# Time mixing from a difference made once a sequence on GpSimd, in a two-layer kernel (time-mixing attention and a mixture of experts)

## The reference

```python
x = x + attn(layernorm(x))      # time mixing, below
x = x + ffn(layernorm(x))       # convolution, 8 experts (top 2), rms norm, gelu feed-forward

xx = pad(x, one token at the front)[:, :-1, :]        # the token ahead
xk = x * time_mix_k + xx * (1.0 - time_mix_k)
xv = x * time_mix_v + xx * (1.0 - time_mix_v)
xr = x * time_mix_r + xx * (1.0 - time_mix_r)
k, v, r = xk @ Wk.T, xv @ Wv.T, xr @ Wr.T
rwkv = sigmoid(r) * wkv(w, time_first, k, v)          # a running, weighted mean over time
return rwkv @ Wo.T
```

## Time and profile before

| What | Value |
|---|---|
| Median of 3 runs | 1038.97 us (1038.87 to 1040.74) |
| Profiled execution, first to last instruction | 1038.4 us |
| TensorE busy | 955.6 us (92%) |
| VectorE busy | 863.5 us (83%) |
| ScalarE busy | 722.8 us (70%) |
| GpSimd busy | 207.7 us (20%) |
| Mean granted TensorE clock | 0.968 |

### The profile page before, as it was taken

How to read it: one execution, slowest core, us unless ns; L and a number is a source line. 1 busy time by engine, 2 the same in 40 slices (tenths; PEclk the granted TensorE clock), 3 DMA queues, 4 the chain that set the end, 5 groups by cost and what they waited for, 6 DMA issues and landing times.

```text
span 1038.4 us, 15789 instructions
## 1 busy us (share of the span) xinstructions
PE 955.6 (92%) x4288; PEld 470.2 (45%) x4288; DVE 863.5 (83%) x1577; ACT 722.8 (70%) x1233; POOL 207.7 (20%) x475
## 2 busy tenths in 40 slices
PE   4536999999999999999999999999999999979895
PEld 2222454454545545454444445444454545344432
DVE  4998889889898988989898888989898997957562
ACT  4664687786868787786868778686877779464532
POOL 3393302121131202112130222113120111101000
PEclk9766999999999999999999999999999999999997
DMA  6110100101010010101010010101001000100000
GB/s 198 42 40 1 41 1 1 62 1 62 0 61 0 23 38 0 61 0 61 0 57 4 0 61 0 61 0 61 0 8 53 19 24 1 41 1 21 1 21 20
DMA packets 28772, 29.66 MB, mean 29 GB/s; under 512 B 2090, under 2 KB 28484, under 8 KB 28484
## 3 DMA queue, kind: packets, MB, share of 16 engines
q1 hardware_dynamic: 28740, 29.27, 8.4%
HBM read 20.87 MB, written 8.39 MB: 28 GB/s over the span
## 4 chain that ended last, share of the span: by engine, by line
PE 81%; DVE 6%; POOL 5%; issue 4%; ACT 3%; DMA 0%; POOLq 0%; DVEq 0%; ACTq 0%; SPq 0%
PE pk L447 15%; PE pe L464 12%; PE pe L466 10%; PE pe L465 10%; PE pe L462 7%; PE po L507 6%; PE po L533 5%; PE pt L441 4%; PE pt L621 3%; POOL msp L408 1%; PE po L504 1%; PE po L501 1%; PE pt L486 1%; DVE comb L1292 1%; ACT sq L746 1%
## 5 line engine op out<-in xcount | busy, mean ns | idle before, releaser
L726 ACT ACTIVATE ye<-pe 128x512 f32<-128x512 f32 x256 | 152.7, 597 | 165.5 <-PE pe L466 152.3
L1292 DVE SCALAR_TENSOR_TENSOR comb<-ye,rw,comb 128x256 f32<-128x256 f32 x448 | 216.3, 483 | 44.9 <-ACT ye L726 30.8
L464 PE MATMUL pe<-weh,x1h 128*128 128x512 f16 x512 | 196.8, 384 | 0.0
L465 PE MATMUL pe<-wel,x1h 128*128 128x512 f16 x512 | 194.0, 379 | 0.0
L466 PE MATMUL pe<-weh,x1l 128*128 128x512 f16 x512 | 194.0, 379 | 0.0
L406 POOL TENSOR_TENSOR msv<-ms,rms_eps_c 128x2 f32<-128x2 f32 x32 | 11.4, 356 | 453.1 <-ACT sq L746 453.1
L462 PE MATMUL pe<-brow,ones 2*128 2x512 f16 x256 | 98.5, 385 | 0.0
L464 PEld LDWEIGHTS pe<-weh,x1h 128*128 128x128 f16 x512 | 49.5, 97 | 88.2 <-issue 58.0
L377 POOL TENSOR_TENSOR mo<-st 128x4 f32<-128x4 f32 x32 | 11.2, 348 | 339.1 <-DVE st L1098 181.8
L466 PEld LDWEIGHTS pe<-weh,x1l 128*128 128x128 f16 x512 | 50.1, 98 | 60.5
L447 PE MATMUL pk<-xk,wa 128*128 128x512 f32 x128 | 65.2, 657 | 11.3 <-issue 8.5
(11 more groups left out here) (152 smaller groups left out, 1946.7 us busy)
## 6 DMA issues: line engine op xcount, KB each, us to landing
xa<-in_x SPq DMA_DIRECT2D x16, 512.0 KB, 3.6
xres<-in_x SPq DMA_DIRECT2D x16, 512.0 KB, 4.4
out_y<-yo SPq DMA_DIRECT2D x16, 512.0 KB, 2.9
ye<-in_w_expert SPq DMA_DIRECT2D x2, 1024.0 KB, 6.7
wa<-in_w_attn SPq DMA_DIRECT2D x1, 1024.0 KB, 7.5
wpw<-in_w_pw SPq DMA_DIRECT2D x1, 256.0 KB, 7.1
wout<-in_w_out SPq DMA_DIRECT2D x1, 256.0 KB, 6.3
wdown<-in_w_down SPq DMA_DIRECT2D x2, 64.0 KB, 5.0
```

The costliest lines, as they stand in the source:

```text
L464: nc.tensor.matmul(dst, x1h[:, h, tok], weh[:, h, cols], start=False, stop=False)
L465: nc.tensor.matmul(dst, x1h[:, h, tok], wel[:, h, cols], start=False, stop=False)
L726: act.activation(ye[:, i % NY, :], pe[:, i % 2, :], ACT.Silu, scale=1.0 / WSCALE).then_inc(ye_ready.sem, 1)
L1292: v.scalar_tensor_tensor(out=comb[:, t, :], in0=src, scalar=rw[:, t, e:e + 1], in1=comb[:, t, :], op0=ALU.mult, op1=ALU.add).then_inc(comb ...
```

## The change

GpSimd subtracts, for each half of each sequence, the token ahead from the token, into a new tile `step`. VectorE's mix then is `step` times the mix weight plus the token ahead, read from `xt1`, and no longer in place. ScalarE's six copies a sequence, the tile `keep` and the semaphores `faded` are gone. The steps stand in GpSimd's list behind the two layer-norm scales; they wait for the halves of `xt1` and, as `step` has one buffer, for all mixes of the sequence before. `mix` now waits itself for the products that read the old xk, xv or xr.

```diff
-        keep = sb("keep", [P, 3, H])
...
+        step = sb("step", [P, H, T])
...
-        faded = [sig("faded_" + m, 2) for m in "kvr"]
+        step_ready = sig("step_ready", 2)
...
-        EARLY_CONST = 5
+        EARLY_CONST = 4
...
+            def steps(seq):
+
+                if on(seq - 1):
+                    pool.wait_ge(mixed.sem, mixed.at(seq - 1))
+                for h in range(H):
+                    pool.wait_ge(xt1_ready.sem, xt1_ready.at(seq, h + 1))
+                    nc.gpsimd.tensor_tensor(step[:, h, :], xt1[:, h, 1:1 + T], xt1[:, h, 0:T],
+                                            ALU.subtract).then_inc(step_ready.sem, 1)
...
                     rstd(b, st2, mo2, pw2, rstd2, shift2, stats2, moments2, rstd2_ready, xn2_ready)
+                if on(n):
+                    steps(n)
                 if on(f):
                     inverse_rms(f, 0)
...
-                def fade(m, h):
-
-                    act.wait_ge(xt1_ready.sem, xt1_ready.at(n, h + 1))
-                    if on(a):
-                        act.wait_ge(kvr_done.sem, kvr_done.at(a, H * (m + 1)))
-                    act.activation((xk, xv, xr)[m][:, h, :], xt1[:, h, 0:T], ACT.Identity,
-                                   scale=keep[:, m, h:h + 1]).then_inc(faded[m].sem, 1)
...
                     copy_front()
-                    fade(0, 0)
-                    fade(0, 1)
                     if on(b):
                         copy_proj()
                         first_tap()
-                    for m in (1, 2):
-                        for h in range(H):
-                            fade(m, h)
                     return
...
-                    if on(n):
-                        fade(0, 0)
                     copy_combined(f, 0)
                     silus(2, (0,))
-                    if on(n):
-                        fade(0, 1)
...
-                    if on(n):
-                        fade(2, 0)
                     silus(3, (2,))
...
-                    if on(n):
-                        fade(1, 0)
-                        fade(1, 1)
-                        fade(2, 1)
                     silus(3, (3,))
...
-            v.tensor_scalar(keep[:], vec[:, 2:5, :], -1.0, 1.0, ALU.mult, ALU.add).then_inc(early_const.sem, 1)
...
                 def mix(seq, m, dst):
 
-                    for h in range(H):
-                        dve.wait_ge(faded[m].sem, faded[m].at(seq, h + 1))
-                        v.scalar_tensor_tensor(out=dst[:, h, :], in0=xt1[:, h, 1:1 + T], scalar=vec[:, 2 + m, h:h + 1],
-                                               in1=dst[:, h, :], op0=ALU.mult, op1=ALU.add).then_inc(mixed.sem, 1)
+                    if on(seq - 1):
+                        dve.wait_ge(kvr_done.sem, kvr_done.at(seq - 1, H * (m + 1)))
+                    for h in range(H):
+                        dve.wait_ge(step_ready.sem, step_ready.at(seq, h + 1))
+                        v.scalar_tensor_tensor(out=dst[:, h, :], in0=step[:, h, :], scalar=vec[:, 2 + m, h:h + 1],
+                                               in1=xt1[:, h, 0:T], op0=ALU.mult, op1=ALU.add).then_inc(mixed.sem, 1)
```

## The result

The changed kernel takes 1044.22 us (median of 4 runs, 1043.52 to 1045.80), the kernel before beside it 1039.61 us (4 runs, 1038.87 to 1040.74). The ratio is 1.0051, with an interval of 1.0036 to 1.0065: slower by about 5 us, more than the 0.2% that tells it from no change. The profiled execution after took 1043.52 us, with a span of 1041.7.

What follows compares the result with a forecast made beforehand. TensorE was taken to bound the steady part, single waits the opening. Nothing in 13 steady iterations, 1.5 us in the first two opening stages and 3.6 in the third sum to 5.1: 1044.1 us, range 1039.5 to 1051.

Steps and rivals of the forecast that it cites:

- The bound: TensorE bounds the steady iterations, with one 1.10 us pause; the opening is a chain of single ScalarE, VectorE and GpSimd waits.
- ScalarE's copies: Six copies a sequence removed, some 4.3 us of ScalarE; worth nothing in the steady part.
- The step's length: A 128x512 subtraction on GpSimd, put between smaller and larger operations by elements: 1.05 us, bounds 0.20 and 3.59.
- What a step does to VectorE: A step stops a two-input VectorE instruction for its whole length: 1.05 us each, 2.1 a sequence.
- a reserve of 2.89 us: Steady part: VectorE's waits, 1.21 us at the last combines and 1.68 at pp, swallow a delay before pp.
- The rival that steps are dear: Steps also cost in the steady part, deciding from 1.7 us a step; at 2.0 us, 1057.6 us; chance 0.12.
- First and second stage: Opening, sequences 0 and 1: xk 0.6 us late in the first; 1.5 us late for both together.
- The wait of the residual for the projection: Second stage: TensorE's projection ends at 57.83, so the residual's second half, at 56.34 before, comes 1.5 us late.
- Third stage: Sequence 2: the expert weights' low parts stand behind steps waiting for xt1; high part ends at 87.75, not 84.12: +3.6 us.
- The sum and its base: 1.5 + 3.6 is 5.1 us; span from 1038.4 to 1043.5, plus 0.6 for the median: 1044.1 us.
- VectorE does not keep its turn: Answers the rival that a ready VectorE goes before waiting GpSimd operations: 5.6 us gained, 1033.4 us; chance 0.10.
- no change to measure: Rival: steps under 0.4 us, or the opening hides the third stage's wait; +0.3 to +2 us, say 1040.5; chance 0.13.

Runs made afterwards that it cites:

- open_by_copies: Changed kernel with the first three sequences mixed by ScalarE's old copies, the other 13 by the step: 1042.54 us, ratio 0.9999 to the kernel before.
- open_by_steps: The first three sequences mixed by the GpSimd step, the other 13 by ScalarE's copies: 1048.35 us, ratio 1.0049 to the kernel before.
- copies_scale_on_act: First three sequences by copies, 13 by the step, GpSimd's multiplications of the expert weights' low parts moved to ScalarE: 1030.79 us, ratio 0.9888 to the kernel before.
- steps_x4: Changed kernel with every step of sequences 3 to 15 made four times: 1076.00 us, ratio 1.0324 to the kernel before.
- first_two_by_steps: Sequences 0 and 1 mixed by the step, sequence 2 and all later ones by ScalarE's copies: 1041.86 us, ratio 1.0018 to the kernel before.
- third_by_steps: Sequences 0 and 1 mixed by ScalarE's copies, sequence 2 and all later ones by the step: 1043.36 us, ratio 1.0028 to the kernel before.
- steps_x2: Changed kernel with every step of sequences 3 to 15 made twice: 1047.23 us, ratio 1.0052 to the kernel before.

## Why the prediction came out right

**The bound.** TensorE in the steady part and single waits in the opening: right. open_by_copies and open_by_steps put the whole loss into the first three sequences. TensorE's only pause was taken as 1.10 us; it can be 1.38, in kernels with and without the step.

**ScalarE's copies.** Counted at nothing in the steady part: right, by open_by_copies and copies_scale_on_act.

**The step's length.** 1.05 us by interpolation: right. The shortest takes 1.03, and three in a row 1.13 each.

**What a step does to VectorE.** Wrong: "a long GpSimd operation stops a two-input VectorE instruction for its whole length" holds for the 128x2048 operations and not for the steps. Eight steps pushed VectorE by 0.70 us each. In the steady part this term stood against a reserve of 2.89 us, in which 1.2 fit as 2.1 would have, so the error cost nothing there. The rival that steps are dear decides, by these rows, from a push of 3.5 us a sequence, five steps of this kind and not two. And what gives first is xk, as steps_x4 shows: pp has no wait left there, and TensorE waits for xk.

**First and second stage.** Mis-sized in its parts. In the first, by the timeline of GpSimd and VectorE after, xk ends at 16.83, 0.5 us later than in the earlier trace rows, where 0.6 was forecast:

```profile
13.59 2.03 POOL L418 TENSOR_TENSOR step<-xt 128x512 f32<-128x512 f32 x2 [4.11 <-ACT xt L802]
...
14.66 2.17 DVE L1067 SCALAR_TENSOR_TENSOR xk<-step,vec,xt 128x512 f32<-128x512 f32 x2 [8.38 <-POOL step L418]
```

In the second, the stops of 0.7 us made xk's product late by 2.0 us (43.81 against 41.81) instead of 2.7; rwkv's wait went, as said. That all of this lateness reaches the projection was wrong in the changed kernel's profile: the product took 5.42 us at a granted clock of 0.67 where it had taken 6.43 at 0.56, and the projection came 1.0 us late. The wait of the residual for the projection, from which 1.5 us came, is there in first_two_by_steps (0.49 us) and absent in the changed kernel's profile. The runs put the two stages at 1.9 us (0.9 to 2.8), which holds the 1.5.

**Third stage.** The term that carries the result, and right in mechanism and size: 87.75 was forecast for the end of the high part with no delay from earlier stages, 87.73 came. That it fits to 0.02 us is luck, as two errors of half a microsecond cancel: the steps ended at 74.25 and not at 73.75, because the first waited until num had ended at 72.36, and the low parts stopped VectorE for less than the whole of their own 7.5 us, as they had before (3.43 and 3.74 us by the earlier trace rows). third_by_steps has 2.9 us (1.9 to 4.1) for the stage.

**The sum and its base.** The sum was 5.1 us; between the medians 4.6 were measured, by the ratio 5.3. The prediction took 0.6 us as what lies around the span, which is the distance of the profiled span to the median. In all four runs of the changed kernel the time is 1.8 us above the span. By that, the profiled execution before was one of about 1040.2 us, 1.2 above the median of 1038.97: the working was right for an execution, and added to the median it assumes that the two have the same opening. That 1044.1 meets the median of 1044.22 to 0.1 us is luck therefore; that the loss is some 5 us, and where it lies, is not. Between the two profiled executions the spans differ by 3.3 us, near the third stage's term alone; the first two stages' part is in other executions, and TensorE's run began where it was forecast, at about 102.3, in open_by_steps and steps_x2 alone.

**The rivals.** VectorE does not keep its turn: the first low part got in between xk's two instructions and the second operation behind them, ahead of the convolution's first, as they had got in at the first ends in the earlier trace rows. The rule of the Trainium skill, SBUF — State Buffer, "Who interferes with whom", that the one who comes second fully blocks, is borne out there by the length of the stop (5.44 us for two instructions of 0.7); beside the steps the measured push of 0.70 us of 1.1 is less than the rule gives, and the measurement decides. That it is no change to measure fell with the ratio's interval.

What stays open: why a short GpSimd operation stops VectorE for less than its length, why executions with the same opening begin TensorE's unbroken run up to 2 us apart, and why TensorE's pause ahead of hh is 1.10 us in some iterations and 1.38 in others.

## What to carry to other kernels

An instruction that is added to an engine's list with a wait delays all that stands behind it there: read that list in the opening too, where the order is not covered by other work. Here two steps of 1 us cost 3.6 us in the third stage's timeline, by the place that they took from a longer operation. GpSimd's operations on two inputs were paid for by VectorE's two-input instructions, the long ones nearly in full. So where a stretch hangs on VectorE, moving a product with a constant to an idle ScalarE (3.6 us on GpSimd, 1.9 on ScalarE; 12 us of the time for two) was worth more than sparing ScalarE some copies. And a difference of a few microseconds between two traces need not be the edit's: compare each kernel with one that ran beside it.

## What the runs showed of the hardware

A 128x512 subtraction on GpSimd takes 1.03 to 1.13 us and pushes a busy VectorE by 0.70 us on average (steps_x4), by 0.58 to 0.69 beside 128x256 combines and by 0.83 where it meets one 128x1024 instruction. A 128x2048 operation beside it pushes VectorE by nearly its whole 3.6 to 3.9 us, 3.43 and 3.74 in the earlier trace rows. Two GpSimd operations on 128x2 beside VectorE's convolution take 1.77 or 2.05 us together, and TensorE's pause that hangs on them 1.10 or 1.38. And a device time lies 1.75 to 1.97 us above the span of its own execution in the runs listed (1.80 to 1.84 in the changed kernel's four), so a profile whose span stands alone belongs to an execution that is longer by that much.
